# Delta rule: the first half of the state's decay as copies on ScalarE, the second half on GpSimd right behind the residuals

## What is computed

```python
def step(S, xs):
    q_t, k_t, v_t, g_t, b_t = xs
    S = S * jnp.exp(g_t)[..., None, None]
    kv = jnp.einsum('bhk,bhkv->bhv', k_t, S)
    S = S + jnp.einsum('bhk,bhv->bhkv', k_t, (v_t - kv) * b_t[..., None])
    o_t = jnp.einsum('bhk,bhkv->bhv', q_t, S)
    return (S, o_t)
```

## Time and profile before

| | us |
|---|---|
| median of 3 runs | 2752.18 |
| lowest and highest of them | 2749.46, 2767.91 |
| the profiled execution | 2759.03 |
| its span in the trace | 2757.3 |
| mean granted clock of TensorE in it | 0.854 |

### The profile page before, as it was taken

The page is one execution under the profiler, slowest core; times in us unless marked ns, Lnnn a source line. Parts: engine busy times, 40 slices in busy tenths (PEclk is TensorE's granted clock), DMA queues, the critical chain, the costliest instruction groups (busy, mean ns, idle before and its releaser), DMA issues. The chain is left out here.

```text
span 2757.3 us, 63709 instructions
## 1 busy us (share of the span) xinstructions
PE 2190.4 (79%) x25656; PEld 1399.2 (51%) x25656; DVE 1861.2 (68%) x4429; ACT 1426.6 (52%) x2901; POOL 779.7 (28%) x845
## 2 busy tenths in 40 slices
PE   2698888889888593459889999889999986587984
PEld 1244444444444372236666666666666654455552
DVE  2477767777765425558898989888888882682433
ACT  0377667667665331156666666666666634131321
POOL 1000001001001132014444444344444442203884
PEclk9599999889987896658998989888888887597997
DMA  5000000000000041200000000000000000443334
GB/s 195 19 1 5 5 5 9 5 5 9 5 5 9 12 127 43 80 9 10 12 12 12 12 12 12 12 12 12 12 12 12 4 5 26 120 123 85 48 44 86
DMA packets 109527, 85.53 MB, mean 31 GB/s; under 512 B 22367, under 2 KB 97283, under 8 KB 108977
## 3 DMA queue, kind: packets, MB, share of 16 engines
q1 hardware_dynamic: 95664, 68.31, 8.4%
q0 software_dynamic: 13568, 13.14, 3.0%
HBM read 59.22 MB, written 22.71 MB: 30 GB/s over the span
## 5 line engine op out<-in xcount | busy, mean ns | idle before, releaser
L617 ACT ACTIVATE Pr<-Pr,nmax 128x512 f32<-128x512 f32 x512 | 341.2, 714 | 179.0 <-DVE nmax L552 176.2
L722 PEld LDWEIGHTS bank<-ident,Pr 128*128 128x128 f32 x2048 | 241.3, 151 | 259.1 <-DVE PT L561 154.8
L722 PE MATMUL bank<-ident,Pr 128*128 128x128 f32 x2048 | 313.5, 296 | 71.5 <-DVE PT L561 59.3
L552 DVE CUSTOM_DVE_ANT_0 Pr<-bank,Tb 128x512 f32<-128x512 f32 x512 | 331.1, 685 | 43.6 <-PE bank L708 43.6
L561 DVE COPY PT<-bank 128x512 f32<-128x512 f32 x256 | 176.5, 689 | 183.6 <-PE bank L736 179.0
L2436 PE MATMUL bank<-Wcv,hw 128*128 128x512 f32 x512 | 272.8, 681 | 8.2 <-POOL hw L1987 5.6
L2177 DVE TENSOR_TENSOR Tc<-Tc,pr 128x30 f32<-128x30 f32 (+14 forms) x480 | 200.5, 418 | 16.5
L624 ACT ACTIVATE PT<-bank 128x512 f32<-128x512 f32 x256 | 150.9, 589 | 110.7 <-PE bank L736 76.5
L2176 DVE TENSOR_TENSOR pr<-AC,Tc 128x30 f32<-128x30 f32 (+14 forms) x480 | 181.4, 378 | 17.4 <-POOL Tc L2051 3.6
L708 PE MATMUL bank<-kp,qp 8*128 8x512 f32 x1024 | 178.9, 697 | 1.1 <-DVE nmax L552 1.1
L2436 PEld LDWEIGHTS bank<-Wcv,hw 128*128 128x128 f32 x512 | 106.2, 219 | 130.4 <-issue 123.6
(11 more groups left out here) (398 smaller groups left out, 4491.8 us busy)
## 6 DMA issues: line engine op xcount, KB each, us to landing
aB<-alpha SPq DMA_DIRECT2D x64, 128.0 KB, 2.8
Tb<-scores SPq DMA_DIRECT2D x1, 7168.0 KB
w<-in_L_ffn_W SPq DMA_DIRECT2D x16, 256.0 KB, 5.4
rawW<-in_L_ffn_up_w SPq DMA_DIRECT2D x16, 256.0 KB, 3.0
rawW<-in_L_ffn_gw SPq DMA_DIRECT2D x16, 256.0 KB, 3.5
rawW<-in_L_ffn_down_w SPq DMA_DIRECT2D x16, 256.0 KB, 4.0
disp<-zero SPq DMA_DIRECT2D x1, 2580.0 KB, 14.6
xin<-disp SPq DMA_DIRECT2D x8, 322.5 KB, 6.3
```

What stands on the lines that cost most here:

```text
L552: V.tensor_tensor_reduce(out=Pr[:, s, i, :], in0=pS[hh][:, :], in1=Tb[:, h, at:at + L], scale=-1.0, scalar=3.0e38, op0=ALU.add, op1=ALU.mi ...
L617: A_(Pr[:, s, i, :], Pr[:, s, i, :], ACT.Exp, scale=-1.0, bias=nmax[:, s, i:i + 1])\
L722: last = TR(pT[m % 2][:, t * P:(t + 1) * P], Pr[:, (G % 2) * HG + hh, t, j * P:(j + 1) * P], ident[:, :])
```

## The change

The first half of S (samples 0 and 1) is now scaled on ScalarE by 16 copies of 128x64, each with one column of GC as its scale, behind `weights(k, 1)`. The second half is scaled on GpSimd as before, but at the place of the first, right behind the residuals, and nothing is left at the later place. The semaphore of the first half is `a_s` (from ScalarE) and, for the zeroing, `g_s0`; `g_s` counts the second half alone. At k = 15 GpSimd zeroes both halves behind the residuals.

```diff
@@ gpsimd
                     for f in range(2):
-                        G.memset(S[:, 2 * f:2 * f + 2, :, :], 0.0).then_inc(s["g_s"], 1)
+                        G.memset(S[:, 2 * f:2 * f + 2, :, :], 0.0).then_inc(s["g_s" if f else "g_s0"], 1)
...
-                    def decay(k, f):
+                    def decay(k):
                         if k == NS - 1:
                             return
                         pool.wait_ge(s["p_qs"], half(k, 1))
-                        Sf = S[:, 2 * f:2 * f + 2, :, :]
+                        Sf = S[:, 2:4, :, :]
                         if k % NCK == NCK - 1:
+                            G.memset(S[:, 0:2, :, :], 0.0).then_inc(s["g_s0"], 1)
                             G.memset(Sf, 0.0).then_inc(s["g_s"], 1)
                         else:
-                            gc = GC[:, k // NCK, k % NCK, 2 * f:2 * f + 2, :, :].rearrange("p x q v -> p (x q v)")
+                            gc = GC[:, k // NCK, k % NCK, 2:4, :, :].rearrange("p x q v -> p (x q v)")
...
                             residual(k, 1)
-                            decay(k, 0)
+                            decay(k)
...
                             initial(m + 1)
-                        if 0 <= k < NS:
-                            decay(k, 1)
@@ vector, update
-                        dve.wait_ge(s["g_s"], half(k, f) + 2)
+                        if f:
+                            dve.wait_ge(s["g_s"], k + 2)
+                        else:
+                            dve.wait_ge(s["a_s"], k - k // NCK + 1)
@@ scalar
+                    def decay(k):
+                        if k % NCK == NCK - 1:
+                            return
+                        act.wait_ge(s["p_qs"], half(k, 1))
+                        for x in range(2):
+                            for q in range(4):
+                                for v in range(2):
+                                    of = S[:, x, q, DK * v:DK * v + DK]
+                                    last = A_(of, of, ACT.Copy, scale=GC[:, k // NCK, k % NCK, x, q, v:v + 1])
+                        last.then_inc(s["a_s"], 1)
...
                             weights(k, 1)
+                            decay(k)
@@ tensor, read_out
                         if k == 0:
-                            pe.wait_ge(s["g_s"], 2)
+                            pe.wait_ge(s["g_s0"], 1)
+                            pe.wait_ge(s["g_s"], 1)
                         elif k % NCK == 0:
-                            pe.wait_ge(s["g_s"], half(k - 1, 1) + 2)
+                            pe.wait_ge(s["g_s0"], 2)
+                            pe.wait_ge(s["g_s"], k + 1)
```

More of the change, by code:

```diff
@@ L1876, in delta1 @@
                         "v_ks", "v_qs", "v_s", "v_o", "v_lt", "v_at", "v_ac", "v_tt", "v_conv", "v_ss",
-                        "v_rn", "v_sr", "v_link", "g_x", "g_s", "g_d1", "g_t", "g_t0", "g_halo", "g_on", "g_hw", "g_ac", "v_nm", "a_kq", "g_ud",
-                        "a_m", "a_w", "a_yp", "a_on", "a_sq", "a_osq", "a_or", "a_lk", "d_al0", "d_al1", "d_out"]) as s:
+                        "v_rn", "v_sr", "v_link", "g_x", "g_s0", "g_s", "g_d1", "g_t", "g_t0", "g_halo", "g_on", "g_hw", "g_ac", "v_nm", "a_kq", "g_ud",
+                        "a_m", "a_w", "a_s", "a_yp", "a_on", "a_sq", "a_osq", "a_or", "a_lk", "d_al0", "d_al1", "d_out"]) as s:
             raw = s.sb("raw", [P, 4, 2, 4, KS - 1 + 2 * CK])
```

## The result

The changed kernel takes 2809.9 us (median of 4 runs, 2793.3 to 2819.4) against 2755.4 for the kernel before, beside it: a ratio of 1.0185, with a 95% interval of 1.0124 to 1.0247. Forecast were 2827 and a slower kernel. The measured time lies inside the forecast range (2783 to 2850), but the size is 54 us against 75.

A forecast was written before the change was run, and what follows sets the result against it. The prediction took ScalarE's queue, then PE, to bound odd steps, with slack in even ones. A 39 us shift plus 36 us of clock gave 75 us on a 2752 us median: 2827 us, range 2783 to 2850.

The forecast's parts named there:

- what bounds the odd step: In an odd step the chain is ACT up to Kt, then PE to the read-out, then the next even Xs.
- The shift: Copies make Kt 3.19 us later in thirteen odd steps: 41.5 us, less 3 us of slack, 39 us.
- the clock term: PE's waits for vt and Kt in odd steps bring the low clock to the tails: 36 us, bounds 0 and 50.
- eight of eleven tails: Of thirteen odd tails two are already low; eight of the other eleven turn low, each costing 4.5 us more.
- The mean tail: Sign: the stretch from Kt to the next read-out near 15 to 16 us, clock near 0.5, in most odd steps.
- Step 15: Taken as nearest case: PE waited 3.17 us for Kt, then the tail took 16.50 us at clock 0.50.
- The holes: PE's waits for vt and for Kt in the odd tail, 2.2 and 2.1 us, almost side by side.
- odd steps end on the ACT chain, so I count it at nothing: GpSimd's removed decay gives VectorE back 0.77 us in each of 14 odd steps, 11 us, counted as no gain.
- the sum: Shift 39 plus clock 36 gives 75 us on the loop's odd steps; even steps cost nothing.
- the wait of Xs: Sign: DVE's wait for the state's read-out (L2459) rises from 24 to about 100 us.
- The new wait: DVE's update of half 0 waits for ScalarE's copies, 0.3 us late in an odd step; cost 0.
- 14 us more: By the skill's clock rule all eleven tails would turn low, making the sum 14 us higher.

The follow-up runs named there:

- e1_spare: Kernel before, both decays kept on GpSimd, plus 16 ScalarE copies at the change's place into a later overwritten part of Kt: ratio 1.0247, loop 1128.7 us.
- e2_even: Changed kernel with ScalarE's copies in even steps only; in odd steps GpSimd scales the first half at the late place: ratio 0.9990, loop 1046.9 us.
- e3_odd: Changed kernel with ScalarE's copies in odd steps only; in even steps GpSimd scales the first half at the late place: ratio 1.0300, loop 1142.4 us.
- e4_early: Changed kernel with ScalarE's copies moved ahead, behind square_out(k - 1, 1), where ScalarE waited for PE: ratio 0.9959, loop 1046.7 us.
- the second profile: Profile of the changed kernel run once more, nothing altered: ratio 1.0205, loop 1108.4 us, odd steps 37.5, even steps 34.6, mean tail 13.4 us.
- e5_fill: Changed kernel plus five unused 128x512 matmuls on PE in odd steps up to 27, before the two gate matmuls: ratio 1.0059, loop 1084.7 us.
- e8_nofirst: Changed kernel without the 16 copies and the wait for them, first half of S not decayed: ratio 0.9936, loop 1042.9 us.

## Why the prediction was right or wrong

**Right: what bounds the odd step, and that ScalarE's queue carries the loss.** `e1_spare` (copies without the rest), `e2_even` and `e3_odd` (by parity) and `e4_early` (another place) all say so. Kt was forecast 3.19 us later and came 3.56 later in the mean. From Ws to Kt it is 3.1 us, close to the forecast. The rest is that, in nine of the thirteen odd steps, Ws itself comes 0.75 us later behind Xs (12.0 instead of 11.2). I read it as part of the gain of the even steps, taken off again (Xs comes early against PE's list), but no run tests that. The shift is thus 13 x 3.56 = 46 us, against 41.5 in the forecast before the slack came off.

**Right in kind, too large: the clock term.** Forecast were 36 us, eight of eleven tails turning to 4.5 us more. The mean tail rose from 12.01 to 14.02, 13 x 2.0 = 26 us, in the second profile 18. The count was too low and the price too high. The second gate pair is at the low clock in all thirteen tails. But only three of them are 16.4 to 16.5 us long, as low as step 15's. The others lie between 12.0 and 14.0: there the clock came back inside the norms, as in step 21 (4.35 us and not 6.93). The loss behind the norms was in most tails before as well, and costs nothing new. `e5_fill` shows that the holes are the cause: with them filled the mean tail is below the 12.0 of the kernel before. Step 15 was the wrong neighbour for the size. The holes weren't those forecast either: 3.00 and 0.86 us in step 21, against 2.2 and 2.1.

**Wrong: "odd steps end on the ACT chain, so I count it at nothing".** That was said of GpSimd's decay that goes. It is true of the odd steps and says nothing of the even ones, which have no such chain and for which the prediction gave no cost of the decay. In the kernel before, the late decay is mostly hidden there: in step 12 it lay beside the update of S from PSUM, and in 5 of 13 steps it held an instruction. The copies push O on ScalarE back, and so the gating multiplications on GpSimd. With the decay still there VectorE is held 33 times in the thirteen even steps by the two together (`e1_spare`), without it 17 times. Beside the copies the release is worth 11 to 16 us of loop behind the update, without them nothing there (`e8_nofirst`). The even steps fell by 1.1 us, 17 us in all (10 us in the second profile), against 0 in the sum. Of the fall about half stands ahead of the update, in PE's chain and its clock (0.78 instead of 0.71), and isn't traced to the release.

So by the profile the sum reads 13 x 5.4 = 70 us for the odd steps (forecast 75), 17 us back in the even ones and 2 in step 15 (forecast 0), which is 51. The measured medians differ by 54. That the odd steps agree so well is partly luck: the shift was 5 us too small and the clock term 10 too large (18 by the second profile). Of the signs that the prediction named, the wait of Xs reached 65.6 us and not 100, and the mean tail 14.0 us and not 15 to 16.

**The new wait** of the update for the copies was forecast 0.3 us late. It is 18.4 us in 13 times, 1.1 to 1.6 each. The 0.77 us by which the late decay had held L2116 are gone, so VectorE arrives earlier: 0.3 and 0.77 make the 1.07 us of the four steps in which Ws comes at 11.2. In the nine others, where Ws is late, it is 1.6. It stays hidden in front of a late Xs, as forecast: `e1_spare` has no such wait and the same odd steps.

**The rules.** That on the shared SBUF interfaces (the Trainium skill, GPSIMD Engine Reference, 8. Key points) names contention with VectorE instructions that have two SBUF inputs. The trace agrees (1.21, 1.36 and 1.27 us for the three substitutions). The prediction weighed it on one row of an odd step and gave it nothing for the even ones. The rule on the clock (the Trainium skill, TensorE: Matmul & The Clock Gate, HAM oscillation — how this bites in real kernels) describes a loop in which each burst behind a wait starts at the low clock. The trace agrees: all thirteen tails do (2.07 or 2.08 us for the second gate pair). What the prediction made of it, 14 us more, did not come, because in ten of the thirteen the clock is back inside the norms (3.8 to 4.5 us).

## What to carry to other kernels

Price work that is added to an engine's list by what is queued behind it up to the next wait, not by the engine's idle share: the same 16 copies moved Kt by 3.6 us in odd steps in one place and by 0.2 in another, ahead of a wait. When work is taken off GpSimd, look at what VectorE does beside it in every kind of step, and do it again for the order that the change itself produces. Where PE waits twice (3.0 and 0.9 us here) in front of a stretch that ends the step, count the clock too, and try unused matmuls in the hole: they gave back 24 of the 51 us of loop here, and 0.5% of the kernel before.

## What the runs showed of the hardware

A wait of PE can cost more than its length: `e5_fill` adds 5 matmuls per odd step to a kernel that is otherwise the same, and is 1.2% faster by the two ratios (1.0059 against 1.0185).

In the rows shown, one GpSimd multiplication holds one VectorE instruction, and to its own end, however short that instruction is (0.20, 0.27 and 0.29 us became 1.21, 1.36 and 1.27 in `e1_spare`). The update of S from PSUM took 1.29 us for two beside the decay, and 1.27 at 1705.48, when that step's decay was over. The substitution behind that update starts at 1573.36, inside the decay (1572.63 to 1574.53), and is held all the same. So what counts in these rows is whether a substitution, with both inputs in SBUF, starts before the multiplication ends. The second gating multiplication of step 22 in the changed kernel (2070.13 to 2071.41) ended beside the update from PSUM, which took its usual 1.28 us, and held nothing.
